# Attention scores as three rounded products, keys split on GpSimd, exponentials scaled on ScalarE

## The chip, the cores and the metric

One core of one Trainium2 chip runs the whole program. The metric is the time of one execution on the device, in microseconds (us). A core has TensorE (matrix products, PE), VectorE (DVE), ScalarE (ACT), GpSimd (POOL) and the queue of SyncE (SP), which here issues every DMA. Each engine runs its own program in order; a wait holds everything behind it on that engine.

## The reference, cut to what matters

The program is a two-layer block over 8 sequences of 100 tokens, 1024 wide, with a context of 361 tokens each. Layer 0: cross attention (16 query heads, 4 key heads, 96 wide; keys are the 361 context tokens and the 100 tokens themselves, 461 in all), then a feed-forward. Layer 1: cross attention (32 query heads, 8 key heads, 128 wide, queries and keys normalised, keys the 361 context tokens, a mask added), then a mixing of four streams. Each attention, cut:

```python
q = (latents @ Wq.T);  k = (hidden @ Wk.T);  v = (hidden @ Wv.T)
scores = jnp.einsum('bkgqd,bksd->bkgqs', q, k) * scale      # scale = HD ** -0.5
attn = jax.nn.softmax(scores.astype(jnp.float32), axis=-1)
out = jnp.einsum('bkgqs,bksd->bkgqd', attn, v);  return out @ Wo.T
```

## The kernel before

Stages follow each other: layer 1's context projections, layer 0's projections, `attend` for layer 0, a layer norm, the feed-forward, a layer norm, `attend` for layer 1, the mixing. The change is in `attend` (line 819) alone, which serves both layers.

**Two forms of product.** Large products are made of three rounded ones: an operand x is held as a rounded part `hi` (type float32r) and a remainder `lo` = x - hi, also rounded, and hi*hi + hi*lo + lo*hi is summed in PSUM (`product`, line 1267). The score product (line 1326), the turning of the probabilities (line 1337) and their product with the values (line 1346) are plain fp32. A plain fp32 product leaves two records in the trace, a rounded one leaves one.

**Tiles and units.** `attend` walks over units u: 32 in layer 0, 64 in layer 1. A unit is one batch and one key group, with four query heads; HB = 4 units share one key group and one half of the tokens. Query tiles (one 512 KB weight tile gives one product of 24 matmuls over 400 tokens) and output tiles (one per unit, two halves) come from DRAM through `w_raw` (RAW = 3 slots), are rounded by GpSimd into `w_hi` (line 1034) and their remainder made by VectorE in `w_lo` (line 1156), both with SPLIT = 4 slots. The first LEAD query products (6 in layer 0, 7 in layer 1) stand ahead of the units.

**The order, written out by hand.** In unit u TensorE runs: turns of chunks 0 and 1, scores of heads 0 and 1 of unit u + 2, the first half of the output product of unit u - 4, in layer 1 the sum of squares (lines 1304 and 1305), turns of the other chunks, the second half, scores of heads 2 and 3 of unit u + 2, once in four units in layer 1 the turning of the square sums (line 1311), the product with the values, and one query product (layer 0: in three of four units; none in the last units). Scores go to two PSUM banks, one per head of a pair, so a pair waits for the reader of the pair before: ScalarE's exponentials in layer 0 (line 1078), VectorE's scale-and-mask in layer 1 (line 1178).
ScalarE in unit u: copy of turned chunk 0 (line 1118), exponentials of heads 0 and 1 of unit u + 2 (line 1078 or 1081), copy of chunk 2, `copy_sums` (line 1105), exponentials of heads 2 and 3, `o_hi` (line 1140), roots (line 1111), `copy_q` (squares at line 1093, the query copy at line 1096).
VectorE in unit u: copy of chunk 1 (line 1203), maxima of the first pair (line 1166 or 1181), accumulating of the output halves (line 1211), maxima of the second pair, `normalise` of unit u + 1 (reciprocal at line 1189, four multiplies at line 1192), `o_lo` (line 1237), `q_scale` (line 1197), the weights' remainders for unit u + 1. In layer 0 the maxima are also multiplied by the score scale (`exp_bias`, line 1169), which is otherwise applied inside the exponential.
GpSimd in unit u: rounding of the weight tiles of unit u + 1, then in layer 1 the squares of the query product of unit u in two operations (lines 1043 and 1046), double buffered.
SP in unit u: keys and values of unit u + 3 (four slots, three DMAs, line 983 or 988 on) once unit u - 1 has read its values, then the weight tiles of unit u + 2, each once the remainder three tiles back is made.

## Time and profile before

| | |
|---|---|
| median of 3 runs | 2779.82 us (2779.24 to 2783.0) |
| the profiled execution | 2777.63 us, its span 2775.8 us |
| mean granted clock of TensorE | 0.949 of full speed |
| busy: PE, PEld, DVE, ACT, POOL | 91%, 76%, 52%, 30%, 19% |
| attention of layer 0 | from 839 to some 1335 us of the span |
| attention of layer 1 | from 1581 to some 2596 us |
| DMA | 217.4 MB, mean 78 GB/s |

The span is the time from the first to the last recorded instruction, 1.8 us less than the execution. PE is the matmul itself, PEld the load of its stationary operand, which the trace records beside it. A matmul's record is longer than the step to the next one, since matmuls are pipelined: steps are read from starts, or from one end to the next. In a timeline, "128*100 128x361" is stationary rows x columns and moving rows x columns; [1.99 <-DVE attend_p L1192] says how long the engine sat idle before and who ended it.

### The profile page before, as it was taken

The numbers are of one execution on the slowest core, as the hardware profiler recorded it, in microseconds if no ns is written. First come the engines' busy times: TensorE is split into PE (matmuls) and PEld (weight loads), VectorE is DVE, ScalarE is ACT, GpSimd is POOL, SyncE is SP. The second block draws the span as 40 slices with busy tenths as digits, with TensorE's granted clock in tenths as the row PEclk, the third lists the DMA queues.
The fourth block names the chain that finished last, engine by engine and source line by source line (L and its number), as shares of the span: only waits on it lengthen the run. The fifth ranks groups of instructions, "written<-read, shape, count | busy, mean of one in ns | idle before, by whom it ended". The sixth has DMA issues, their size and how long they took to land. (4 is left out here: it accounts for less than half of the span.)

```text
span 2775.8 us, 32483 instructions
## 1 busy us (share of the span) xinstructions
PE 2517.4 (91%) x12384; PEld 2109.7 (76%) x12384; DVE 1455.6 (52%) x2473; ACT 827.3 (30%) x1922; POOL 533.8 (19%) x414
## 2 busy tenths in 40 slices
PE   8999999799996899998769689999999999998824
PEld 6888888589995677776569468888888888886723
DVE  6222222223102576667543546666666766766697
ACT  3222222223212333333210234333333333332323
POOL 3000000000002122211021143334334334331120
PEclk9999999899997999999989889999999999999766
DMA  6222222253222222222021113323323223322001
GB/s 197 69 69 69 69 69 62 74 173 105 68 90 85 62 79 88 80 70 61 12 69 39 55 58 95 103 84 102 101 85 103 95 90 103 93 78 75 9 0 48
DMA packets 159357, 217.40 MB, mean 78 GB/s; under 512 B 31511, under 2 KB 124083, under 8 KB 158179
## 3 DMA queue, kind: packets, MB, share of 16 engines
q1 hardware_dynamic: 159202, 215.33, 25.4%
q8 instruction: 99, 1.62, 0.2%
q14 instruction: 56, 0.45, 0.1%
HBM read 176.99 MB, written 38.29 MB: 78 GB/s over the span
## 5 line engine op out<-in xcount | busy, mean ns | idle before, releaser
L1034 POOL TENSOR_TENSOR attend_w_hi<-attend_w_raw,attend_one 128x1024 fp32r<-128x1024 f32 (+1 forms) x184 | 335.9, 1840 | 478.6 <-DMA attend_w_raw<-in_wo 284.6
L1326 PE MATMUL attend_ps_score<-attend_k_in,attend_q 128*100 128x361 f32 (+1 forms) x768 | 298.1, 512 | 18.6 <-ACT attend_p L1078 11.0
L1271 PE MATMUL attend_ps_gemm<-normed_hi,attend_w_hi 128*128 128x400 f32 x704 | 268.3, 381 | 39.0 <-DVE attend_w_lo L1156 39.0
L1271 PE MATMUL attend_ps_gemm<-attend_o_hi,attend_w_hi 128*128 128x400 f32 x704 | 274.0, 389 | 27.0 <-DVE attend_w_lo L1156 24.5
L1156 DVE TENSOR_TENSOR attend_w_lo<-attend_w_raw,attend_w_hi 128x1024 fp32r<-128x1024 f32 (+1 forms) x184 | 216.7, 1212 | 155.8 <-POOL attend_w_hi L1034 154.8
L1081 ACT ACTIVATE attend_p<-attend_p,attend_neg_max 100x361 f32<-100x361 f32 x256 | 150.8, 590 | 398.0 <-DVE attend_neg_max L1181 398.0
L1271 PE MATMUL attend_ps_gemm<-attend_o_hi,attend_w_lo 128*128 128x400 f32 x704 | 244.7, 348 | 0.0
L1271 PE MATMUL attend_ps_gemm<-normed_lo,attend_w_hi 128*128 128x400 f32 x704 | 244.4, 347 | 0.0
L1271 PE MATMUL attend_ps_gemm<-attend_o_lo,attend_w_hi 128*128 128x400 f32 x704 | 244.2, 347 | 0.0
L1271 PE MATMUL attend_ps_gemm<-normed_hi,attend_w_lo 128*128 128x400 f32 x704 | 243.5, 346 | 0.0
L1211 DVE SCALAR_TENSOR_TENSOR stream_tokens<-attend_ps_gemm,attend_gate,stream_tokens 128x400 f32<-128x400 f32 x192 | 121.4, 633 | 230.3 <-PE attend_ps_gemm L1271 229.7
L1346 PE MATMUL attend_ps_out<-attend_pt,attend_v_in 121*128 121x400 f32 (+4 forms) x640 | 233.9, 503 | 0.0
L301 DVE TENSOR_TENSOR context_k_square<-context_k_rows 128x512 f32<-128x512 f32 (+1 forms) x46 | 31.8, 691 | 346.5 <-ACT context_k_rows L226 346.4
L1326 PEld LDWEIGHTS attend_ps_score<-attend_k_in,attend_q 128*100 128x100 f32 (+1 forms) x768 | 122.6, 171 | 93.2 <-issue 30.9
L1337 PEld LDWEIGHTS attend_ps_turn<-attend_ident,attend_p 100*121 100x121 f32 (+2 forms) x1280 | 167.3, 183 | 29.3 <-issue 9.6
L1346 PEld LDWEIGHTS attend_ps_out<-attend_pt,attend_v_in 121*128 121x128 f32 (+4 forms) x640 | 114.2, 180 | 98.1 <-issue 48.5
L1337 PE MATMUL attend_ps_turn<-attend_ident,attend_p 100*121 100x100 f32 (+2 forms) x1280 | 171.8, 271 | 7.4 <-DVE attend_p L1192 5.5
L1271 PEld LDWEIGHTS attend_ps_gemm<-normed_hi,attend_w_hi 128*128 128x128 f32 x704 | 134.0, 190 | 52.3 <-issue 43.3
L1271 PEld LDWEIGHTS attend_ps_gemm<-attend_o_hi,attend_w_hi 128*128 128x128 f32 x704 | 133.7, 190 | 50.6 <-DVE attend_w_lo L1156 39.7
L1043 POOL TENSOR_TENSOR attend_square_hi<-attend_q_square,attend_one 128x400 fp32r<-128x400 f32 x64 | 57.2, 893 | 550.9 <-ACT attend_q_square L1093 550.8
L350 PE MATMUL context_ps_rows<-context_wk_hi,context_ctx_hi 128*128 128x512 f32 (+1 forms) x368 | 145.9, 396 | 9.9 <-DVE context_wk_lo L294 9.9
L1178 DVE SCALAR_TENSOR_TENSOR attend_p<-attend_ps_score,attend_q_scale,attend_mask 100x361 f32<-100x361 f32 x256 | 147.7, 593 | 11.8 <-PE attend_ps_score L1326 4.6
(252 smaller groups left out, 5071.4 us busy)
## 6 DMA issues: line engine op xcount, KB each, us to landing
attend_w_raw<-in_wq SPq DMA_DIRECT2D x88, 512.0 KB, 3.8
attend_w_raw<-in_wo SPq DMA_DIRECT2D x64, 512.0 KB, 5.1
attend_w_raw<-in_wo SPq DMA_DIRECT2D x32, 384.0 KB, 3.5
context_ctx_raw<-in_ctxT SPq DMA_DIRECT2D x8, 1456.0 KB
attend_k_in<-scratch_k SPq DMA_DIRECT2D x64, 180.5 KB
context_ctx_raw<-in_ctxF SPq DMA_DIRECT2D x22, 512.0 KB
scratch_v<-context_v_out SPq DMA_DIRECT2D x44, 256.0 KB, 2.2
scratch_k<-context_kt_out SPq DMA_DIRECT2D x44, 256.0 KB, 5.0
```

The lines of the kernel that those rows point to most:

```text
L301: dve.tensor_tensor(k_square[:n], part, part, ALU.mult).then_inc(squared, 1)
L350: mm = pe.matmul(ps_rows[:n, m % ROW_BANKS], x[:, t % CTX, c, 0:n], w[:, c, col], start=(c == 0 and x is ctx_hi and w is w_hi), stop=(c == ...
L1034: pool.tensor_tensor(hi, w_flat(w_raw, j % RAW, j), one[:hi.shape[0]].to_broadcast(hi.shape), ALU.mult).then_inc(w_hi_done, 1)
L1043: pool.tensor_tensor(square_hi[:, n % 2], q_square[:], one[:HD].to_broadcast([HD, HT]), ALU.mult).then_inc(square_split, 1)
L1081: act.activation(p[:, slot, h], p[:, slot, h], ACT.Exp, bias=neg_max[:, slot, h:h + 1], accum_out=exp_sum[:, slot, h:h + 1]).then_inc(expe ...
L1156: dve.tensor_tensor(w_flat(w_lo, j % SPLIT, j), w_flat(w_raw, j % RAW, j), w_flat(w_hi, j % SPLIT, j).bitcast(F32), ALU.subtract).then_inc ...
L1178: dve.scalar_tensor_tensor(p[:, slot, h], ps_score[:S, h % 2, :NK], q_scale[:, i % 2, k, h:h + 1], mask[:], ALU.mult, ALU.add).then_inc(s_ ...
L1211: dve.scalar_tensor_tensor(tokens[:, m, at], ps_gemm[:, gemm_at["o", u, half] % 2, :HT], gate[:], tokens[:, m, at], ALU.mult, ALU.add).the ...
L1271: mm = pe.matmul(out, left[a](c), right[b](c), start=(c == 0 and a == b == 0), stop=(c == chunks - 1 and a == 1))
L1326: pe.matmul(ps_score[:S, h % 2, :NK], q[:, i % 2, h, k * S:(k + 1) * S], k_in[:, u % KV_SLOTS], start=True, stop=True).then_inc(s_done, 1)
L1337: turn = pe.transpose(ps_turn[:ROWS[kc], kc % 2, h * S:(h + 1) * S], p[:, u % P_SLOTS, h, at:at + ROWS[kc]], ident[:S, :S])
L1346: mm = pe.matmul(ps_out[:HD, :HG * S], v_in[:ROWS[kc], u % KV_SLOTS, kc], pt[:ROWS[kc], u % 2, kc], start=(kc == 0), stop=(kc == NCH - 1))
```

## The change

Scores become three rounded products (hi*hi, hi*lo, lo*hi) over one column more than there are keys (362 and 462, the last one zero and never read). ScalarE rounds the queries as it copies them (`q_hi`), VectorE makes their remainder (`remainder_q`), at the end of the unit; the PSUM bank of a query product is free only after it. In layer 0 the score scale goes into both, so the exponential has neither scale nor `exp_bias`. GpSimd splits the keys in two operations (`split_keys`), ahead of the unit's weights. The four multiplies of `normalise` go from VectorE to ScalarE, behind the copy of chunk 2; VectorE keeps the reciprocal (`invert`), now behind its copy of chunk 1. Slots: weights split 3 rather than 4, raw weights 3 in layer 0 and 2 in layer 1, keys 2, values 3, squares 1. Keys and values have DMAs and waits of their own. Declarations and semaphores are left out below.

```diff
--- before.py
+++ after.py
...
+    NKE = NK + 1
...
-    RAW, SPLIT = 3, 4
-    P_SLOTS, KV_SLOTS = 3, 4
-    KV_DMAS = 3
+    RAW, SPLIT = 3 - layer, 3
+    P_SLOTS, K_SLOTS, V_SLOTS = 3, 2, 3
+    V_DMAS = 2
...
-        q = sb("q", [HD, 2, HG, HT])
+        q_hi = sb("q_hi", [HD, 2, HG, HT], F32R)
+        q_lo = sb("q_lo", [HD, 2, HG, HT], F32R)
...
-        k_in = sb("k_in", [HD, KV_SLOTS, NK])
-        v_in = sb("v_in", [KR, KV_SLOTS, NCH, HD])
+        k_raw = sb("k_raw", [HD, K_SLOTS, NKE])
+        k_hi = sb("k_hi", [HD, K_SLOTS, NKE], F32R)
+        k_lo = sb("k_lo", [HD, K_SLOTS, NKE], F32R)
+        v_in = sb("v_in", [KR, V_SLOTS, NCH, HD])
...
-        exp_bias = sb("exp_bias", [S, P_SLOTS, HG])
...
-            square_hi = sb("square_hi", [HD, 2, HT], F32R)
-            square_lo = sb("square_lo", [HD, 2, HT], F32R)
+            square_hi = sb("square_hi", [HD, HT], F32R)
+            square_lo = sb("square_lo", [HD, HT], F32R)
...
+            def keys(u):
...
+                b, slot = batch(u), u % K_SLOTS
+                if u >= K_SLOTS:
+                    sp.wait_ge(k_lo_done, u - K_SLOTS + 1)
+                src = k_dram[g][:, b, :] if layer == 0 else k_dram[g][:, b * KEYS:(b + 1) * KEYS]
+                sp.dma_start(k_raw[:, slot, 0:NK], src).then_inc(k_load[slot], 16)
...
+            def values(u):
...
+                b, slot = batch(u), u % V_SLOTS
+                if u >= V_SLOTS:
+                    sp.wait_ge(pv_done, u - V_SLOTS + 1)
...
-            for u in range(KV_SLOTS - 1):
-                kv(u)
+            for u in range(K_SLOTS):
+                keys(u)
+            for u in range(V_SLOTS - 1):
+                values(u)
...
+            keys(K_SLOTS)
             for u in range(NU):
-                kv(u + KV_SLOTS - 1)
+                keys(u + K_SLOTS + 1)
+                values(u + V_SLOTS - 1)
                 for j in step_tiles(u + 2):
                     tile(j)
...
+            pool.memset(k_raw[:, :, NK:NKE], 0.0).then_inc(consts, 1)
...
+            def split_keys(u):
+                if u >= NU:
+                    return
+                slot = u % K_SLOTS
+                pool.wait_ge(k_load[slot], (u // K_SLOTS + 1) * 16)
+                if u >= K_SLOTS:
+                    pool.wait_ge(s_done, (u - K_SLOTS + 1) * HG)
+                pool.tensor_tensor(k_hi[:, slot], k_raw[:, slot], one[:HD].to_broadcast([HD, NKE]), ALU.mult
+                                   ).then_inc(k_hi_done, 1)
+                pool.wait_ge(k_hi_done, u + 1)
+                pool.tensor_tensor(k_lo[:, slot], k_raw[:, slot], k_hi[:, slot].bitcast(F32), ALU.subtract
+                                   ).then_inc(k_lo_done, 1)
...
-                if n >= 2:
-                    pool.wait_ge(q_summed, n - 1)
-                pool.tensor_tensor(square_hi[:, n % 2], q_square[:], one[:HD].to_broadcast([HD, HT]), ALU.mult
+                if n:
+                    pool.wait_ge(q_summed, n)
+                pool.tensor_tensor(square_hi[:], q_square[:], one[:HD].to_broadcast([HD, HT]), ALU.mult
                                    ).then_inc(square_split, 1)
                 pool.wait_ge(square_split, 2 * n + 1)
-                pool.tensor_tensor(square_lo[:, n % 2], q_square[:], square_hi[:, n % 2].bitcast(F32), ALU.subtract
+                pool.tensor_tensor(square_lo[:], q_square[:], square_hi[:].bitcast(F32), ALU.subtract
                                    ).then_inc(square_split, 1)
...
             for j in range(LEAD):
                 weights(j)
                 if j >= SPLIT - 1:
                     squares(j - SPLIT + 1)
+            split_keys(0)
             for n in range(LEAD - SPLIT + 1, LEAD):
                 squares(n)
+            split_keys(1)
             for j in step_tiles(0):
                 weights(j)
+            split_keys(2)
             for u in range(NU):
+                split_keys(u + 3)
                 for j in step_tiles(u + 1):
                     weights(j)
                 squares(query_of(u))
...
-                act.wait_ge(biased if layer == 0 else maxed, 2 * u + pair + 1)
...
-                        act.activation(p[:, slot, h], ps_score[:S, h % 2, :NK], ACT.Exp, bias=exp_bias[:, slot, h:h + 1],
-                                       scale=SCALE, accum_out=exp_sum[:, slot, h:h + 1]).then_inc(exped, 1)
+                        act.activation(p[:, slot, h], ps_score[:S, h % 2, :NK], ACT.Exp, bias=neg_max[:, slot, h:h + 1],
+                                       accum_out=exp_sum[:, slot, h:h + 1]).then_inc(exped, 1)
...
+            def normalise(u):
+                if u >= NU:
+                    return
+                slot = u % P_SLOTS
+                act.wait_ge(inverted, u + 1)
+                for h in range(HG):
+                    act.activation(p[:, slot, h], p[:, slot, h], ACT.Copy, scale=exp_inv[:, slot, h:h + 1]
+                                   ).then_inc(p_ready, 1)
...
-                act.activation(q[:, i % 2, h], ps_gemm[:HD, bank, :HT], ACT.Copy).then_inc(q_read, 1)
                 if layer == 0:
-                    act.activation(q[h * REST:(h + 1) * REST, i % 2, HG - 1], ps_gemm[HD:P, bank, :HT], ACT.Copy
-                                   ).then_inc(q_read, 1)
+                    act.activation(q_hi[:, i % 2, h], ps_gemm[:HD, bank, :HT], ACT.Copy, scale=SCALE).then_inc(q_read, 1)
+                    act.activation(q_hi[h * REST:(h + 1) * REST, i % 2, HG - 1], ps_gemm[HD:P, bank, :HT], ACT.Copy,
+                                   scale=SCALE).then_inc(q_read, 1)
+                else:
+                    act.activation(q_hi[:, i % 2, h], ps_gemm[:HD, bank, :HT], ACT.Copy).then_inc(q_read, 1)
...
-            for u in range(2):
-                exps(u, 0)
-                exps(u, 1)
+            exps(0, 0)
+            exps(0, 1)
+            exps(1, 0)
+            normalise(0)
+            exps(1, 1)
             for u in range(NU):
                 i, k = u // HB, u % HB
                 copy_turn(u, 0)
                 exps(u + 2, 0)
                 copy_turn(u, 2)
+                normalise(u + 1)
                 if layer == 1 and k == 1 and u + HB < NU:
                     copy_sums(i + 1)
                 exps(u + 2, 1)
...
+            def remainder_q(n):
+                if n is None:
+                    return
+                i, h = n // QT, n % QT
+                bank = gemm_at["q", n, 0] % 2
+                dve.wait_ge(q_read, (n + 1) * Q_COPIES)
+                if layer == 0:
+                    last = slice(h * REST, (h + 1) * REST)
+                    dve.scalar_tensor_tensor(q_lo[:, i % 2, h], ps_gemm[:HD, bank, :HT], SCALE,
+                                             q_hi[:, i % 2, h].bitcast(F32), ALU.mult, ALU.subtract).then_inc(q_lo_done, 1)
+                    dve.scalar_tensor_tensor(q_lo[last, i % 2, HG - 1], ps_gemm[HD:P, bank, :HT], SCALE,
+                                             q_hi[last, i % 2, HG - 1].bitcast(F32), ALU.mult, ALU.subtract
+                                             ).then_inc(q_lo_done, 1)
+                else:
+                    dve.tensor_tensor(q_lo[:, i % 2, h], ps_gemm[:HD, bank, :HT], q_hi[:, i % 2, h].bitcast(F32),
+                                      ALU.subtract).then_inc(q_lo_done, 1)
...
-                    dve.wait_ge(maxed, 2 * u + pair + 1)
-                    dve.tensor_scalar(exp_bias[:, slot, heads], neg_max[:, slot, heads], SCALE, None, ALU.mult
-                                      ).then_inc(biased, 1)
...
-            def normalise(u):
+            def invert(u):
...
                 dve.wait_ge(exped, (u + 1) * HG)
                 dve.reciprocal(exp_inv[:, slot], exp_sum[:, slot]).then_inc(inverted, 1)
-                dve.wait_ge(inverted, u + 1)
-                for h in range(HG):
-                    dve.tensor_scalar(p[:, slot, h], p[:, slot, h], exp_inv[:, slot, h:h + 1], None, ALU.mult
-                                      ).then_inc(p_ready, 1)
...
-            for j in range(LEAD):
+            for j in range(SPLIT):
                 split(j)
+            for j in range(SPLIT, LEAD):
+                remainder_q(j - SPLIT)
+                split(j)
+            for n in range(LEAD - SPLIT, LEAD):
+                remainder_q(n)
             if layer == 1:
                 scales(0)
             for j in step_tiles(0):
                 split(j)
-            for u in range(2):
-                maxima(u, 0)
-                maxima(u, 1)
-            normalise(0)
+            maxima(0, 0)
+            maxima(0, 1)
+            maxima(1, 0)
+            invert(0)
+            maxima(1, 1)
             for u in range(NU):
                 i, k = u // HB, u % HB
                 copy_turn(u, 1)
+                invert(u + 1)
                 maxima(u + 2, 0)
                 if u >= HB:
                     accumulate(u - HB, 0)
...
                 maxima(u + 2, 1)
-                normalise(u + 1)
...
                 for j in step_tiles(u + 1):
                     split(j)
+                remainder_q(query_of(u))
...
-                        pe.wait_ge(q_read, (at + 1) * Q_COPIES)
+                        pe.wait_ge(q_lo_done, (at + 1) * Q_COPIES)
...
-                    pe.wait_ge(kv_load[u % KV_SLOTS], (u // KV_SLOTS + 1) * 16 * KV_DMAS)
+                    pe.wait_ge(k_lo_done, u + 1)
                     if k == 0:
-                        pe.wait_ge(q_read, (i + 1) * QT * Q_COPIES)
+                        pe.wait_ge(q_lo_done, (i + 1) * QT * Q_COPIES)
...
-                    pe.matmul(ps_score[:S, h % 2, :NK], q[:, i % 2, h, k * S:(k + 1) * S], k_in[:, u % KV_SLOTS],
-                              start=True, stop=True).then_inc(s_done, 1)
+                    at = slice(k * S, (k + 1) * S)
+                    for a, b in ((q_hi, k_hi), (q_hi, k_lo), (q_lo, k_hi)):
+                        mm = pe.matmul(ps_score[:S, h % 2, :NKE], a[:, i % 2, h, at], b[:, u % K_SLOTS],
+                                       start=(a is q_hi and b is k_hi), stop=(a is q_lo))
+                    mm.then_inc(s_done, 1)
...
+                pe.wait_ge(v_load[u % V_SLOTS], (u // V_SLOTS + 1) * 16 * V_DMAS)
```

## Rows read from the trace of the kernel before

**Rows 1.** The page, part 1: busy us (share) xinstructions of each engine.

```profile
PE 2517.4 (91%) x12384; PEld 2109.7 (76%) x12384; DVE 1455.6 (52%) x2473; ACT 827.3 (30%) x1922; POOL 533.8 (19%) x414
```

**Rows 2.** Busy us of PE, PEld, DVE, ACT, POOL by stretch; clock; DMA.

```profile
970.00:1240.00 270.00, 266.14 (x1288) 205.43 (x1287) 189.57 (x356) 103.30 (x293) 54.61 (x33) 1.00 0.28 82
1700.00:2500.00 800.00, 799.78 (x4114) 678.93 (x4112) 548.19 (x925) 296.46 (x751) 295.98 (x212) 1.00 0.30 94
```

**Rows 3.** TensorE's waits, and who ended them: us, times, longest.

```profile
PE attend_ps_gemm L1271 <- DVE attend_w_lo L1156: 63.5, 19, 25.9
```

**Rows 4.** Timeline, units of layer 1: start us, us, engine, line, operation.

```profile
2008.22 0.99 PE L1337 MATMUL attend_ps_turn<-attend_ident,attend_p 100*121 100x100 f32 x8
...
2008.83 0.50 ACT L1096 ACTIVATE attend_q<-attend_ps_gemm 128x400 f32<-128x400 f32 x1
...
2009.06 1.38 PE L1326 MATMUL attend_ps_score<-attend_k_in,attend_q 128*100 128x361 f32 x4
...
2009.26 0.57 DVE L1203 COPY attend_pt<-attend_ps_turn 121x400 f32<-121x400 f32 x1 [1.13 <-PE attend_ps_turn L1337]
...
2011.10 0.91 DVE L1181 TENSOR_REDUCE attend_neg_max<-attend_p 100x2 f32<-100x722 f32 x1
...
2013.84 0.48 ACT L1105 ACTIVATE attend_q_sum<-attend_ps_sum 4x400 f32<-4x400 f32 x1
...
2016.76 0.35 PE L1311 MATMUL attend_ps_sum<-attend_ident,attend_q_sum 4*100 4x4 f32 x4
...
2486.10 0.99 PE L1337 MATMUL attend_ps_turn<-attend_ident,attend_p 100*121 100x100 f32 x8
```

**Rows 5.** Timeline, a pair of scores of layer 0, the product ahead.

```profile
1002.52 0.34 PE L1271 MATMUL attend_ps_gemm<-attend_o_hi,attend_w_lo 128*128 128x400 f32 x1
1002.70 1.71 PE L1326 MATMUL attend_ps_score<-attend_k_in,attend_q 96*100 96x461 f32 x4
```

**Rows 6.** Timeline, rounded products of 512, 362 and 384 columns, first and last counted.

```profile
399.76 0.39 PE L350 MATMUL context_ps_rows<-context_wk_hi,context_ctx_hi 128*128 128x512 f32 x1
...
401.80 0.39 PE L350 MATMUL context_ps_rows<-context_wk_hi,context_ctx_hi 128*128 128x512 f32 x1
...
726.19 0.33 PE L765 MATMUL context_ps_out<-context_ctx_hi,context_wk_hi 128*128 128x362 f32 x1
...
729.83 0.33 PE L765 MATMUL context_ps_out<-context_ctx_lo,context_wk_hi 128*128 128x362 f32 x1
...
814.66 0.34 PE L765 MATMUL context_ps_out<-context_wv_hi,normed_hi 128*100 128x384 f32 x1
...
816.23 0.34 PE L765 MATMUL context_ps_out<-context_wv_hi,normed_hi 128*100 128x384 f32 x1
...
814.84 0.16 PEld L765 LDWEIGHTS context_ps_out<-context_wv_hi,normed_lo 128*100 128x100 f32 x1
```

**Rows 7.** Groups by line: xcount | busy us, mean ns | idle; exponentials.

```profile
L1081 ACT ACTIVATE attend_p<-attend_p,attend_neg_max 100x361 f32<-100x361 f32 x256 | 150.8, 590 | 398.0 <-DVE attend_neg_max L1181 398.0
```

**Rows 8.** The same groups, GpSimd's rounding of weights, remainder of squares.

```profile
L1034 POOL TENSOR_TENSOR attend_w_hi<-attend_w_raw,attend_one 128x1024 fp32r<-128x1024 f32 x152 | 288.8, 1917 | 255.4 <-DMA attend_w_raw<-in_wq 166.2 <-DMA attend_w_raw<-in_wo 63.0 <-PE attend_ps_gemm L1271 26.0
L1046 POOL TENSOR_TENSOR attend_square_lo<-attend_q_square,attend_square_hi 128x400 fp32r<-128x400 f32 x64 | 67.3, 1051 | 5.0
```

**Rows 9.** DMA issues: xcount, KB each, median us from issue to landing.

```profile
attend_w_raw<-in_wo SPq DMA_DIRECT2D x64, 512.0 KB, 5.1
```

**Rows 10.** Timeline, a unit without a query product ahead of it.

```profile
2498.40 1.38 PE L1326 MATMUL attend_ps_score<-attend_k_in,attend_q 128*100 128x361 f32 x4
...
2499.74 1.16 DVE L1156 TENSOR_TENSOR attend_w_lo<-attend_w_raw,attend_w_hi 128x1024 fp32r<-128x1024 f32 x1
```

**Rows 11.** Timeline, first scores and turns of layer 0, with idle ahead.

```profile
889.79 3.39 PE L1326 MATMUL attend_ps_score<-attend_k_in,attend_q 96*100 96x461 f32 x4 [2.18 <-ACT attend_p L1078]
...
895.17 2.44 PE L1337 MATMUL attend_ps_turn<-attend_ident,attend_p 100*121 100x100 f32 x8 [1.99 <-DVE attend_p L1192]
```

**Rows 12.** VectorE's split of the weights: duration ns min/median/max.

```profile
L1156 DVE TENSOR_TENSOR attend_w_lo<-attend_w_raw,attend_w_hi x184: 950/1215/2909, 845.4 to 2570.8; 128x1024 fp32r<-128x1024 f32 x152, 128x768 fp32r<-128x768 f32 x32
```

29 lines of the change are left out of this document (15 added, 14 removed).

## The prediction

> **What bounds the kernel now.** I read the page's busy times first: TensorE is busy 2517 us of 2776 [rows 1]. That is an average over stages, so next come the busy times by stretch. In the middle of layer 1's attention TensorE is busy 799.78 us of 800 at a granted clock of 1.00; in the middle of layer 0's, 266.14 of 270 [rows 2]. VectorE is at 69%, ScalarE at 37% and GpSimd at 37% in the 800 us. So each us taken out of TensorE's stream there is a us of the kernel, unless an in-order queue elsewhere turns late. The list of TensorE's waits says which: weights' remainders (line 1156), 63.5 us in 19 waits, one of 25.9 at the start of the stage, the rest in starts and in units without a query product [rows 3]. A unit is one batch and one key group; from the turns at 2008.22 to those of the 32nd unit after, at 2486.10, it takes 14.93 us [rows 4].
>
> **Scores, the large term.** Before, a head is one fp32 product, recorded as two. In layer 1 the turns end at 2008.22 + 0.99 = 2009.21 and the four records of a pair of heads at 2009.06 + 1.38 = 2010.44: 1.23 us a pair [rows 4]. In layer 0 (461 keys) the product ahead ends at 1002.52 + 0.34 = 1002.86 and the pair at 1002.70 + 1.71 = 1004.41: 1.55 us [rows 5].
> After, a head is three products of rounded operands, over 362 or 462 columns. No score runs so yet, but the same kind does in the projections. At 362 columns the starts go from 726.19 to 729.83 in 22 steps: 0.1655 us each; at 512, 399.76 to 401.80 in 9: 0.227; a line between them gives 0.206 at 462 [rows 6]. So a pair is 6 x 0.1655 = 0.99 us in layer 1 and 6 x 0.206 = 1.24 us in layer 0. Gain: 0.24 x 128 pairs = 30 us, of which I take 0.23 and 29 us, since starts are given to 0.01; and 0.31 x 64 pairs = 19.8 us. **Sum 48.8 us**. Between bounds: the 512 row's own price for layer 0 gives 1.36 a pair and 12 us; the 362 row's 0.99 gives 36.
> Here a rule speaks against the change. The rows show products with 100 stationary columns, rounded, over 384 moving ones, every 0.1744 us (814.66 to 816.23 in 9 steps), each with a weight load of its own [rows 6]. So the third load per head (one per record before) is hidden, and I add nothing.
> The Trainium skill, TensorE: Matmul & The Clock Gate, in its list of what overlaps under the measured speedup of tiles, has a weight load overlap a product in flight only where their row groups differ. By its section on LDWEIGHTS 100 columns would then cost 83 ns a product, and 1152 products an estimated 96 us, less those loads that fp32 exposes today. By that rule, these rows disagree.
>
> **Normalising moves from VectorE to ScalarE.** Four multiplies a unit leave VectorE. ScalarE gets four copies of 100x361: at most the exponential's 0.59 us on the same tile [rows 7], at least the 0.48 of a small copy [rows 4], less what neighbours overlap: some 2 us a unit, on an engine at 37%. What waits behind them counts: the second exponentials, which wait for later scores anyway, and in layer 1 once in four units the copy of the square sums, which TensorE reads to turn (line 1311). In the unit at 2008.22 it starts 5.6 us into the unit and TensorE arrives at 8.54 [rows 4]. After, the query remainder holds VectorE's turn copy by some 0.6, and through maxima and exponentials this copy too; then the four copies: start 8.2 to 8.7, end 8.6 to 9.2. TensorE arrives 0.46 earlier, at 8.08. Wait 0 to 1.1 us, taken 0.6, 15 times: **9 us given back** (0 to 17).
>
> **Query remainders on VectorE**, one per query product in layer 1, two in layer 0: 0.57 us each by the copy of the same size [rows 4]. VectorE loses 1.4 to 1.6 us of multiplies a unit against that. They sit at the unit's end and start once ScalarE has rounded, 1.1 us into the next unit, so VectorE's turn copy comes at 1.7 rather than 1.04, and the maxima of the first pair end near 4.4. TensorE asks for their buffers at 7.2: hidden. In layer 0, two exponentials end near 5.5 and are wanted at 6.4: hidden, by 1 us. The gemm bank is wanted two products on.
>
> **Keys split by GpSimd**: two operations a unit; over 128x400 the dearer of such operations costs 1.05 us [rows 8], so over 362 columns the two take at most 1.9, over 462 some 2.4. With two squares' operations at up to 1.05 and two weight tiles at 1.92 [rows 8] GpSimd goes from 5.9 of 14.9 us to 7.8 of 14.5. They are a whole unit ahead of the scores that read them. Behind them stand the weights of the next unit. With three rounded slots for four, the query tile's rounding now waits for the output product of the running unit, 7.2 us in; it ends at 9.1. VectorE splits it some 12 us into the unit, once the products' remainder is done: hidden by some 3 us.
>
> **One raw slot less (layer 1) and the loads.** On SP's queue the tile loads of a unit go out after VectorE's splits at the unit's end, land 5.1 us later [rows 9], and keys and values stand behind them. Keys, a third of the bytes, land 5 to 6 us into the next unit, their split ends near 8, the output tile's rounding near 10, the query tile's near 12: hidden by 1 to 3 us. Values have a unit and more; their three slots suffice, since a slot's reader is two units back.
>
> **Where the stream waits for a weight remainder anyway**, a quicker first pair gains nothing: in the unit at 2497 the scores end at 2499.78 and the remainder at 2500.90 [rows 10]. There are some 12 such units in layer 0 (8 first units of a token half, 4 at the end) and 5 in layer 1: 12 x 0.31 + 5 x 0.23 = **4.8 us back**.
>
> **Starts.** Layer 0's first score pairs run at about half clock, 3.39 us each with ScalarE between, and the first turns wait 1.99 for the multiplies [rows 11]. Four pairs at half clock save some 0.6 more than counted, the bias operation 0.2 each, the earlier normalising 1: **4 us gained** (0 to 6). Layer 1: the second key split (1.9 us) precedes the weight rounding for which the first maxima wait; half-clock scores save about half: **1 us lost**. Memset, reciprocal moved, squares in one buffer: nothing; the squares' readers come 1 us later than their writers today.
>
> Sum: -48.8 + 9 + 4.8 - 4 + 1 = -38 us. From the profiled execution's 2777.6, 2739.6; the runs' median is 2.2 above it, so **2742 us**.
>
> **Rivals.**
> A, *nothing given back* (2729 us, 2721 to 2733): ScalarE's copies take 0.4, so the square sums come in time; for it, neighbouring ScalarE rows overlap by 0.1. 48.8 + 4 - 1 = 52 at best.
> B, *ScalarE and VectorE run late* (2762, 2752 to 2775): the wait at line 1311 is 1.1 (8 us more) and layer 0's second pair waits 0.5 us for the first pair's exponentials in its 24 query units (12 more): 20 above the forecast. For it, the 1 us of slack.
> C, *the weight chain becomes the bound* (slower, 2799): in layer 1 with two raw slots the chain from one unit's split to the next is in series: landing 5.1, keys' landing 1.7 (a third of the bytes), key split 1.9, rounding 1.9, split 1.2: 11.8 of 14.5 us. But VectorE's split ran up to 2.91 rather than 1.2 beside a GpSimd operation [rows 12]. With 2.9 each for rounding and split and half as much again for the keys the chain is 15.5: 1.0 us a unit over 57 units, 57 us. It decides against the change from 15.2 on, where it takes back the 38. Against it: most splits took the median 1.215.
> The Trainium skill, SBUF — State Buffer, on the shared port pair, says that a VectorE operation with two SBUF inputs and a GpSimd operation that reads SBUF shut each other out for a whole instruction; the 2.91 agrees.
> D, *weight loads show* (2914): were each load's 0.16 us added [rows 6], a head would take 3 x (0.1655 + 0.16) = 0.98 for 0.615 in layer 1 (93 us more) and 1.10 for 0.775 in layer 0 (41 more).
> E, *the rounded product is not the quick form here*: no gain, within 0.2% of before.
>
> **Chances.** Forecast (2733 to 2752) 0.56, A 0.20, B 0.14, C 0.07, D 0.01, E 0.02. The range 2722 to 2765 takes in A and most of B. 0.2% (5.6 us) is about what a measurement of this kernel can tell from no change: faster 0.90, same 0.02, slower 0.08.
>
> **What would show it.** Score records 1152 for 768, starts 0.165 and 0.206 apart; layer 1's unit near 14.5 us; a TensorE wait at the turning of the square sums; first-pair stalls on weight remainders longer by 0.2 to 0.3. Wrong if TensorE's busy share in 1700 to 2450 falls under 97% with GpSimd or the weight remainder named, or if the records stand 0.2 apart in layer 1.

## The result, and the profile after

The changed kernel takes **2770.66 us** (median of 8 runs, 2768.73 to 2776.78) against 2779.65 (8 runs, 2777.85 to 2783.0) for the kernel before: ratio 0.9968, 95% interval 0.9958 to 0.9977. It is faster by 9 us; the forecast was 38, and 2770.66 lies above the range of 2722 to 2765. The profiled execution spans 2766.9 us, against 2775.8 before.

From the page, busy times of the engines:

```profile
PE 2489.0 (90%) x12768; PEld 2191.2 (79%) x12768; DVE 1335.7 (48%) x2137; ACT 1018.3 (37%) x2306; POOL 714.3 (26%) x608
```

TensorE's busy time fell by 28 us, the span by 9. Busy times by stretch as in [rows 2], PE, PEld, DVE, ACT, POOL, then the clock, then the DMA:

```profile
970.00:1240.00 270.00, 263.65 (x1405) 225.96 (x1405) 163.63 (x278) 149.46 (x375) 97.69 (x74) 0.99 0.29 84
1700.00:2500.00 800.00, 794.91 (x4432) 728.60 (x4431) 500.86 (x787) 405.53 (x991) 402.43 (x328) 1.00 0.32 98
```

TensorE's waits, as in [rows 3], more of the list: total in us, times, longest.

```profile
PE attend_ps_gemm L1338 <- DVE attend_w_lo L1206: 74.6, 22, 24.6
...
PE attend_ps_gemm L1338 <- DVE stream_tokens L1271: 7.8, 2, 4.3
...
PE attend_ps_sum L1378 <- ACT attend_q_sum L1152: 3.9, 3, 3.6
```

The wait for weight remainders grew from 63.5 us in 19 [rows 3]. The scores themselves did what was forecast. TensorE's timeline, a pair of layer 1 and the product behind it:

```profile
2004.56 0.99 PE L1407 MATMUL attend_ps_turn<-attend_ident,attend_p 100*121 100x100 f32 x8
2005.33 0.39 PE L1395 MATMUL attend_ps_score<-attend_k_hi,attend_q_hi 128*100 128x362 f32 x1
2005.55 0.32 PE L1395 MATMUL attend_ps_score<-attend_k_lo,attend_q_hi 128*100 128x362 f32 x1
...
2006.20 0.32 PE L1395 MATMUL attend_ps_score<-attend_k_hi,attend_q_lo 128*100 128x362 f32 x1
2006.37 0.35 PE L1338 MATMUL attend_ps_gemm<-attend_o_hi,attend_w_hi 128*128 128x400 f32 x1
```

From the second on, the starts are 0.16 apart; the turns end at 2005.55, the pair at 2006.52: 0.97 us for the forecast 0.99. A steady unit of layer 1 takes 14.38 us for 14.84 before.

**Where the rest went** is seen by cutting both traces at the first and the last turns of each layer. Layer 0's units (31 between them) take 427.1 us for 429.4; layer 1's (63) take 891.5 for 908.0. Behind the first turns of each layer's last unit more time passes than before: in layer 0 to the start of the feed-forward stage 80.3 for 72.5 us, in layer 1 to the first product of the mixing 39.8 for 35.2. So layer 0 gained 2.3 us in its units and lost 7.8 behind them.

The trace shows what happens in the units; what stands behind them is taken up with e1_slots. TensorE's timeline in a unit of layer 0 behind one without a query product:

```profile
1260.12 0.37 PE L1395 MATMUL attend_ps_score<-attend_k_hi,attend_q_lo 96*100 96x462 f32 x1
1262.07 0.45 PE L1338 MATMUL attend_ps_gemm<-attend_o_hi,attend_w_hi 128*128 128x400 f32 x1 [1.58 <-DVE attend_w_lo L1206]
...
1262.73 0.36 PE L1338 MATMUL attend_ps_gemm<-attend_o_hi,attend_w_hi 128*128 128x400 f32 x1
1262.91 0.52 PE L1338 MATMUL attend_ps_gemm<-attend_o_lo,attend_w_hi 128*128 128x400 f32 x1
1263.22 0.54 PE L1338 MATMUL attend_ps_gemm<-attend_o_hi,attend_w_lo 128*128 128x400 f32 x1
1263.56 0.54 PE L1338 MATMUL attend_ps_gemm<-attend_o_hi,attend_w_hi 128*128 128x400 f32 x1
...
1266.35 0.35 PE L1338 MATMUL attend_ps_gemm<-attend_o_lo,attend_w_hi 128*128 128x400 f32 x1
1266.54 0.34 PE L1338 MATMUL attend_ps_gemm<-attend_o_hi,attend_w_lo 128*128 128x400 f32 x1
```

The same place in the kernel before:

```profile
1267.28 0.45 PE L1271 MATMUL attend_ps_gemm<-attend_o_hi,attend_w_hi 128*128 128x400 f32 x1 [0.94 <-DVE attend_w_lo L1156]
1267.57 0.34 PE L1271 MATMUL attend_ps_gemm<-attend_o_lo,attend_w_hi 128*128 128x400 f32 x1
1267.75 0.34 PE L1271 MATMUL attend_ps_gemm<-attend_o_hi,attend_w_lo 128*128 128x400 f32 x1
```

Two things changed. The stall grew from 0.94 to 1.58 us, and from 1262.91 on, 0.84 us behind its end, the products start 0.33 apart for 0.18: TensorE is at 1.2 GHz for some 3.4 us. That unit takes 13.53 us where the ones without the drop take 11.92 and the same unit before 12.22. So the stall gives back one pair's gain, and a drop 1.6 us more. Of the ten such stalls in layer 0, five are followed by a drop. From 838 to 1350 us TensorE has 83.7 us at half clock, for 51.2 before. Of the 32.5 us more, 17 stand behind those five stalls and most of the rest at the layer's end.

### The profile page after: what moved, and what is told of

It is laid out like the page before. It is cut to its first block and busy times, and to the rows that moved or that the text cites. A ratio compares the mean times of both kernels' runs of the same rounds, so it can differ in the third digit from the quotient of the medians.

```text
span 2766.9 us, 33590 instructions
## 1 busy us (share of the span) xinstructions
PE 2489.0 (90%) x12768; PEld 2191.2 (79%) x12768; DVE 1335.7 (48%) x2137; ACT 1018.3 (37%) x2306; POOL 714.3 (26%) x608
## 5 line engine op out<-in xcount | busy, mean ns | idle before, releaser
L1338 PE MATMUL attend_ps_gemm<-attend_o_hi,attend_w_hi 128*128 128x400 f32 x704 | 259.0, 368 | 44.7 <-DVE attend_w_lo L1206 36.9
L1417 PE MATMUL attend_ps_out<-attend_pt,attend_v_in 121*128 121x400 f32 (+4 forms) x640 | 239.8, 514 | 0.0
L1126 ACT ACTIVATE attend_p<-attend_p,attend_exp_inv 100x361 f32<-100x361 f32 (+1 forms) x384 | 207.4, 616 | 0.0
L1063 POOL TENSOR_TENSOR attend_k_hi<-attend_k_raw,attend_one 128x362 fp32r<-128x362 f32 (+1 forms) x96 | 81.1, 845 | 445.1 <-DMA attend_k_raw<-scratch_k 291.7
L1395 PE MATMUL attend_ps_score<-attend_k_hi,attend_q_hi 128*100 128x362 f32 (+1 forms) x384 | 141.8, 369 | 21.2 <-ACT attend_p L1114 13.3
L1303 DVE TENSOR_TENSOR attend_o_lo<-attend_ps_out,attend_o_hi 128x400 fp32r<-128x400 f32 (+1 forms) x96 | 51.7, 539 | 216.2 <-ACT attend_o_hi L1190 119.9
```

What stands on the lines that cost most here:

```text
L1063: pool.tensor_tensor(k_hi[:, slot], k_raw[:, slot], one[:HD].to_broadcast([HD, NKE]), ALU.mult).then_inc(k_hi_done, 1)
L1126: act.activation(p[:, slot, h], p[:, slot, h], ACT.Copy, scale=exp_inv[:, slot, h:h + 1]).then_inc(p_ready, 1)
L1303: dve.tensor_tensor(o_lo[:HD, i % 2, :, k * S:(k + 1) * S], ps_out[:HD, :QT * S].rearrange("p (h t) -> p h t", h=QT), o_hi[:HD, i % 2, :, ...
L1338: mm = pe.matmul(out, left[a](c), right[b](c), start=(c == 0 and a == b == 0), stop=(c == chunks - 1 and a == 1))
L1395: mm = pe.matmul(ps_score[:S, h % 2, :NKE], a[:, i % 2, h, at], b[:, u % K_SLOTS], start=(a is q_hi and b is k_hi), stop=(a is q_lo))
L1417: mm = pe.matmul(ps_out[:HD, :HG * S], v_in[:ROWS[kc], u % V_SLOTS, kc], pt[:ROWS[kc], u % 2, kc], start=(kc == 0), stop=(kc == NCH - 1))
```

## The experiments

Ratios are to the kernel before, with their 95% intervals; its median stood at 2779.65 in the runs above and at 2781.26, 2781.23, 2780.70 and 2780.73 in the four sets below. Experiments of different sets are compared with the changed kernel by ratio. The ratios are those on record; the quotients of the medians differ from them by up to 0.0006 (1.6 us). One execution of each kernel was traced, so a difference of one or two us in a single trace can be the clock's.

| label | median us | ratio | 95% |
|---|---|---|---|
| e1_slots | 2789.54 | 1.0025 | 1.0016 to 1.0034 |
| e2_normalise | 2787.44 | 1.0020 | 1.0011 to 1.0029 |
| e3_fp32 | 2795.43 | 1.0048 | 1.0035 to 1.0062 |
| e4_early | 2723.81 | 0.9788 | 0.9774 to 0.9801 |
| e5_before_early | 2758.31 | 0.9917 | 0.9903 to 0.9930 |
| e6_filler | 2755.82 | 0.9911 | 0.9897 to 0.9924 |
| e7_sums | 2716.38 | 0.9766 | 0.9752 to 0.9779 |
| e8_tail | 2717.13 | 0.9770 | 0.9756 to 0.9783 |
| e9_all | 2712.39 | 0.9750 | 0.9735 to 0.9764 |
| e10_defer | 2709.82 | 0.9741 | 0.9726 to 0.9755 |
| e11_fp32_early | 2757.01 | 0.9909 | 0.9893 to 0.9926 |
| e12_stall | 2799.12 | 1.0064 | 1.0050 to 1.0077 |

### Parts of the change alone: e1_slots, e2_normalise, e3_fp32

```diff
--- e1_slots, on the kernel before
-    RAW, SPLIT = 3, 4
+    RAW, SPLIT = 3 - layer, 3
...
```

> The kernel before with three rounded weight slots for four in both layers and two raw ones for three in layer 1, nothing else. Theory 'fewer slots delay the stage ends': the last output tiles wait for a product's slot, TensorE's last waits grow from 1.1 and 1.3 us to some 3.4 and 4.3, and with them the tails: 5 to 12 us slower than the kernel before. Rival 'slots hidden', as the prediction had it: within 2 us. Rival 'the layer 1 loads come late too': more than 20 us slower, with weight waits inside layer 1's steady units.

0.25% of 2780 is 7 us slower: the first theory. Steady units are as before (14.85), so the third rival falls. GpSimd's timeline at the end of layer 0, then TensorE's:

```profile
1347.99 1.47 POOL L1034 TENSOR_TENSOR attend_w_hi<-attend_w_raw,attend_one 128x768 fp32r<-128x768 f32 x1 [11.22 <-PE attend_ps_gemm L1271]
```

```profile
1351.26 0.67 PE L1271 MATMUL attend_ps_gemm<-attend_o_hi,attend_w_hi 128*128 128x400 f32 x1 [3.42 <-DVE stream_tokens L1211]
```

In the kernel before that rounding was released by the load, not by a product:

```profile
1342.04 1.47 POOL L1034 TENSOR_TENSOR attend_w_hi<-attend_w_raw,attend_one 128x768 fp32r<-128x768 f32 x1 [9.07 <-DMA attend_w_raw<-in_wo]
```

With three slots the last tile waits until the last but three is multiplied. The trace puts the stall down to the accumulation (line 1211); the changed kernel, with stalls of 3.42 us in layer 0 and 4.33 in layer 1 (where e1_slots has 5.95), shows what was late. Its timeline at the end of layer 1, GpSimd, VectorE, TensorE:

```profile
2555.23 2.23 POOL L1053 TENSOR_TENSOR attend_w_hi<-attend_w_raw,attend_one 128x1024 fp32r<-128x1024 f32 x1 [0.77 <-PE attend_ps_gemm L1338]
2557.50 1.22 DVE L1206 TENSOR_TENSOR attend_w_lo<-attend_w_raw,attend_w_hi 128x1024 fp32r<-128x1024 f32 x1 [1.78 <-POOL attend_w_hi L1053]
2558.65 1.17 DVE L1271 SCALAR_TENSOR_TENSOR stream_tokens<-attend_ps_gemm,attend_gate,stream_tokens 128x400 f32<-128x400 f32 x2
...
2559.42 0.42 PE L1338 MATMUL attend_ps_gemm<-attend_o_hi,attend_w_hi 128*128 128x400 f32 x1 [4.33 <-DVE stream_tokens L1271]
```

VectorE's queue has all four splits ahead of the accumulations, so the accumulation that frees TensorE's bank stands behind a split that waits for a late rounding. The slots alone account for what layer 0 loses behind its units: from the first turns of its last unit to the layer norm's first product it is 40.3 us here, 40.4 in the changed kernel and 32.6 before. Half clock from 1310 us to that product is 20.5 us in both, for 6.8 before.

```diff
--- e2_normalise, on the kernel before (ScalarE's order; VectorE keeps the reciprocal, behind copy_turn(u, 1))
                 copy_turn(u, 2)
+                normalise(u + 1)
...
```

> The kernel before with the normalising alone moved to ScalarE, in the changed kernel's order. The prediction's step: waits at the turning of the square sums of 0.6 us 15 times (9 us) less what the starts gain, so 5 us slower. By the trace of the changed kernel the waits are 0.46 us, so about 4 us slower, within 2 us. Rival 'ScalarE is where the gain went': 15 us or more slower. Rival 'free': the same within 1 us.

0.20%: 5.6 us slower, near the forecast of 5, but not where the forecast had it. The units in which the square sums are turned take 15.31 us as before: no wait there in steady state. The loss is in layer 1's second unit (16.36 for 12.71, a wait of 2.9 us at the turning with half clock behind it), partly offset by its first (11.93 for 13.55), in layer 0's first two units (33.8 for 31.9) and in layer 1's last (11.68 for 9.74). And the stall on the weight remainder is 1.29 us, not 0.94, at an equal unit length of 12.22. The reason shows in the turns ahead of it. The kernel before, TensorE and its weight loads:

```profile
1263.45 1.33 PE L1337 MATMUL attend_ps_turn<-attend_ident,attend_p 100*121 100x100 f32 x8
...
1264.01 0.60 PEld L1337 LDWEIGHTS attend_ps_turn<-attend_ident,attend_p 100*121 100x121 f32 x5 [0.19 <-DVE attend_p L1192]
```

and e2_normalise:

```profile
1264.57 0.99 PE L1346 MATMUL attend_ps_turn<-attend_ident,attend_p 100*121 100x100 f32 x8
```

VectorE's multiplies used to hold the turns back by 0.34 us. Freed, TensorE comes that much earlier to a remainder that is no earlier.

```diff
--- e3_fp32, on the changed kernel
-                    for a, b in ((q_hi, k_hi), (q_hi, k_lo), (q_lo, k_hi)):
-                        mm = pe.matmul(ps_score[:S, h % 2, :NKE], a[...], b[...], ...)
+                    mm = pe.matmul(ps_score[:S, h % 2, :NK], q_hi[...].bitcast(F32), k_hi[...].bitcast(F32),
+                                   start=True, stop=True)
```

> The changed kernel with each score one fp32 product of the rounded halves again (it leaves out the remainders' part of the scores), all else kept. If rounded scores are worth the predicted 48.8 less 4.8 in this order of work: 2813 to 2817 us. If layer 0's share is given back through stalls (weight remainders and the clock behind them), only layer 1's 57 units of 0.46 count: 26 us, 2795 to 2800. If the gain in layer 1 is lost as well: below 2785.

Everything but the rounded scores costs 0.48%, 13.4 us, of which slots (7.0) and normalising (5.6) alone make 12.6: keys on GpSimd and the query remainders are free within the intervals. The rounded scores are worth 1.0048 - 0.9968, 22 us, in the changed kernel: the second theory's size or a little less. The stalls are 1.28 to 1.29 us here, and none of the ten brings a drop.

### The late remainder: e4_early and e5_before_early

VectorE sits idle ahead of o_lo while the rounded weights have been ready for long. VectorE's rows in the changed kernel:

```profile
1259.69 0.47 DVE L1303 TENSOR_TENSOR attend_o_lo<-attend_ps_out,attend_o_hi 96x300 fp32r<-96x300 f32 x1 [2.82 <-ACT attend_o_hi L1194]
...
1261.06 0.96 DVE L1206 TENSOR_TENSOR attend_w_lo<-attend_w_raw,attend_w_hi 128x768 fp32r<-128x768 f32 x1
```

```diff
--- e4_early, on the changed kernel (e5_before_early: the same, on the kernel before)
                 maxima(u + 2, 1)
+                early = step_tiles(u + 1)[:1] if u + 1 >= HB else []
+                for j in early:
+                    split(j)
                 dve.wait_ge(o_hi_done, (u + 1) * O_COPIES)
...
-                for j in step_tiles(u + 1):
+                for j in step_tiles(u + 1)[len(early):]:
                     split(j)
```

> The changed kernel with VectorE's remainder of the next output tile placed ahead of its wait for ScalarE's rounded outputs, not behind. Theory 'the chain from values through o_hi and o_lo to the weight remainder bounds the units without a query product, and stalls of 1.6 us bring half clock': the 1.58 us waits fall to 0.4 to 0.7, the half-clock stretches behind them go away, 15 to 25 us faster than the changed kernel: 2746 to 2756. Rival 'the clock drops for another reason': only the waits shrink, 16 x 1.0: 2754 to 2760 with the half-clock stretches still there. Rival 'the wait moves to another engine': within 4 us of 2771.

It is 0.0180 of 2780, 50 us, faster than the changed kernel by ratio (the two traces differ by 44), twice what was expected. VectorE's rows in e4_early, one unit:

```profile
1256.56 0.95 DVE L1206 TENSOR_TENSOR attend_w_lo<-attend_w_raw,attend_w_hi 128x768 fp32r<-128x768 f32 x1
...
1259.46 0.47 DVE L1306 TENSOR_TENSOR attend_o_lo<-attend_ps_out,attend_o_hi 96x300 fp32r<-96x300 f32 x1 [1.96 <-ACT attend_o_hi L1194]
```

and TensorE's waits there:

```profile
PE attend_ps_gemm L1341 <- DVE attend_w_lo L1206: 37.7, 2, 24.8
...
PE attend_ps_turn L1410 <- DVE attend_pt L1263: 5.8, 10, 2.0
```

Twenty of 22 waits are gone from this list (at the layers' last tiles waits of 2.7 and 1.25 us stay, which the trace puts down to no engine), and units with output products only take 10.09 us in layer 0 for 11.92 or 13.53, 9.63 in layer 1 for 11.15. What I had left out of the expectation: a remainder that isn't late gives back all of the stall, and the half clock, and the pair that the stall used to swallow. The units of layer 0, first to last turns, take 400.6 us for 427.1, layer 1's 881.5 for 891.5.

> The kernel before with the same reordering as e4_early and nothing of the change: the remainder of the next output tile ahead of VectorE's wait for the rounded outputs. It has 17 waits of some 0.94 us there, so it gains 16 to 19 us and comes to 2762 to 2766. The change is then worth about 38 to 42 us between the two reordered kernels, as the prediction's sum had it, and what the change lost was lost to the weight remainders. Rival 'the reordering is as good for either kernel': it too gains 47 us, 2734, and the change is worth only 9 whatever the order.

22.9 us faster than the kernel before, a little more than expected. Between the two reordered kernels the change is worth 2758.31 - 2723.81 = **34.5 us**: near the sum of 38. The second rival (9 whatever the order) falls.

### The clock: e6_filler and e12_stall

```diff
--- e6_filler, on the changed kernel, ahead of the wait for w_lo in outputs()
                 if half == 0:
+                    if layer == 0 and query_of(u + HB - 1) is None and u + HB > HB:
+                        for _ in range(7):
+                            pe.matmul(ps_sum[:, :HT], ln_hi[:, 0, 0:P], ln_hi[:, 0, 0:HT], start=True, stop=True)
                     pe.wait_ge(w_lo_done, j + 1)
```

> The changed kernel with seven extra rounded products (about 1.2 us, into a bank that layer 0 does not use) in each of layer 0's stalls of 1.58 us on a weight remainder; no wait is taken away. Theory 'the stall brings the half clock': the half-clock stretches behind those stalls go away and the kernel is 12 to 18 us faster than the changed one (2753 to 2759) though it does more work. Rival 'the half clock has another cause': as many half-clock stretches, within 2 us of 2771 or slower.

16 us faster by ratio (0.0057), with more work. The condition holds in 16 places, and the trace has 112 filler products: seven ahead of each of the ten stalls, and as many in each of six places at the layer's end. TensorE's timeline:

```profile
1254.85 1.43 PE L1358 MATMUL attend_ps_sum<-normed_hi 128*128 128x400 f32 x7
1256.58 0.45 PE L1338 MATMUL attend_ps_gemm<-attend_o_hi,attend_w_hi 128*128 128x400 f32 x1 [0.31 <-DVE attend_w_lo L1206]
1256.88 0.35 PE L1338 MATMUL attend_ps_gemm<-attend_o_lo,attend_w_hi 128*128 128x400 f32 x1
1257.06 0.34 PE L1338 MATMUL attend_ps_gemm<-attend_o_hi,attend_w_lo 128*128 128x400 f32 x1
```

The product behind the wait starts no earlier in its unit (3.82 us behind the turns in both), but no half-clock products follow, in none of the ten places; half clock in the stage falls from 83.7 to 51.2 us, as before the change. Half of the difference is 16 us, about the gain. But not all of that is the price of the drops behind the ten stalls. The traces differ by 8 us in the five units that had a drop (1.6 each), by some 6 at the layer's end (1.6 in its last unit, 4.7 behind it), where e1_slots has as much half clock as the changed kernel, and by less than 1 elsewhere. The stretch 1240 to 1300 us in the changed kernel and in e6_filler, columns as above:

```profile
1240.00:1300.00 60.00, 53.14 (x250) 41.77 (x248) 30.25 (x54) 34.46 (x88) 15.62 (x13) 0.91 0.19 50
```

```profile
1240.00:1300.00 60.00, 58.40 (x308) 47.04 (x307) 34.10 (x60) 35.48 (x93) 17.09 (x14) 1.00 0.23 64
```

```diff
--- e12_stall, on the kernel before, VectorE
                 dve.wait_ge(o_hi_done, (u + 1) * O_COPIES)
+                if layer == 0 and u >= HB and query_of(u) is None:
...
+                    for t in range(2):
+                        dve.tensor_tensor(waste[:, t, 0:QT * S], ps_out[:HD, :QT * S], one[:HD].to_broadcast([HD, QT * S]),
+                                          ALU.mult).then_inc(waste_done, 1)
```

> The kernel before with two extra VectorE products (96x300, about 0.47 us each, into a tile that nothing reads) between ScalarE's rounded outputs and the weight remainder, in layer 0's 13 units without a query product. The 10 waits of 0.94 us become some 1.9 us, with nothing of the change in the kernel. Theory 'a longer stall lowers the clock': half-clock stretches of 3.4 us stand behind most of them, each 1.6 us dearer than the wait alone: 13 x 0.95 = 12 us and 7 to 10 times 1.6, together 24 to 28 us, 2804 to 2809. Rival 'the clock falls by what the change computes, not by the stall': 10 to 13 us slower only, 2791 to 2794, with the half-clock time in layer 0 as before.

18 us slower: between the two. The stalls are 1.70 us, for 0.94, in all ten places (0.76 each, 10 us over 13 units), but in the profiled execution only two of the ten were followed by a drop; the longer ones at the stage's end (3.25, 3.59 and 4.42 us) all were, and half clock rose from 51.2 to 71.7 us (here up to 1363 us, since the stage ends later). TensorE's rows, first without a drop behind it, then with one:

```profile
1301.40 0.45 PE L1281 MATMUL attend_ps_gemm<-attend_o_hi,attend_w_hi 128*128 128x400 f32 x1 [1.70 <-DVE attend_w_lo L1159]
...
1314.37 0.52 PE L1281 MATMUL attend_ps_gemm<-attend_o_hi,attend_w_hi 128*128 128x400 f32 x1 [1.70 <-DVE attend_w_lo L1159]
```

So stalls bring the drops without anything of the change, but the length alone doesn't settle one near 1.6 us. Fewer drops came than the theory had forecast. What else decides there is open.

### The other terms: e7_sums, e8_tail, e11_fp32_early

```diff
--- e7_sums, on e4_early, ScalarE
-                normalise(u + 1)
                 if layer == 1 and k == 1 and u + HB < NU:
                     copy_sums(i + 1)
+                normalise(u + 1)
```

> e4_early with ScalarE's copy of the square sums ahead of its normalising, not behind. The prediction gave 9 us to this wait at the turning of the square sums; the trace of the changed kernel shows 0.46 us at 13 places. Theory: 5 to 8 us faster than e4_early, 2716 to 2719. Rival 'the wait moves to the next reader' (the exponentials or the maxima behind them): within 1.5 us of 2724.

7.4 us faster, of which the traces place 5.7. Units that turn the square sums take 14.83 us for 15.05 (14 times, 3 us), and layer 1's second unit 14.81 for 17.55. That unit was the dearest single spot. The 0.46 us in the expectation is the step from the product ahead to the turning, not a wait: TensorE is idle there for 0.14 us, and the step is 0.25 in e7_sums (0.40 in the kernel before). TensorE's rows in it, in the kernel before and in the changed one:

```profile
1664.74 0.35 PE L1311 MATMUL attend_ps_sum<-attend_ident,attend_q_sum 4*100 4x4 f32 x4 [0.96 <-ACT attend_q_sum L1105]
```

```profile
1667.31 0.50 PE L1378 MATMUL attend_ps_sum<-attend_ident,attend_q_sum 4*100 4x4 f32 x4 [3.55 <-ACT attend_q_sum L1152]
1667.74 1.04 PE L1417 MATMUL attend_ps_out<-attend_pt,attend_v_in 121*128 121x400 f32 x1
```

There the four copies sit between the sums and their reader while no output products cover them, and half clock follows (1.04 us for the first product, which takes 0.60 in the kernel before).

```diff
--- e8_tail, on e4_early: the last 2 * HB tiles take slots out of four, the fourth in the query buffers
+            if j == len(tiles) - 2 * HB:
+                users[SPLIT] = -SPLIT
...
+            flat = w[:, slot] if slot < SPLIT else spare[:, 0].rearrange("p h t -> p (h t)")
...
+                elif slots[j][0] == SPLIT:
+                    pool.wait_ge(s_done, (NU - HB) * HG)
```

> e4_early with a fourth rounding slot for the last eight output tiles of each layer, in the half of the query buffers whose scores are done. Theory 'the missing slot delays the stage ends': the last waits of TensorE in each layer shrink by some 2 to 3 us, 4 to 8 us faster than e4_early, 2716 to 2720. Rival 'the loads of the last tiles bound the end, not the slots': within 1.5 us of 2724.

6.7 us faster, what e1_slots had lost. Layer 0's stall on the accumulation is gone; layer 1's stays at 4.37 us, so there the rounding slot is not the last cause. GpSimd's rows in e8_tail show the last rounding of layer 1 released by the load of its tile, where the changed kernel had a product:

```profile
2502.79 2.36 POOL L1067 TENSOR_TENSOR attend_w_hi<-attend_w_raw,attend_one 128x1024 fp32r<-128x1024 f32 x1 [0.65 <-DMA attend_w_raw<-in_wo]
```

Layer 1 has two raw slots for three, but that wasn't tried alone.

> e4_early with each score one fp32 product of the rounded halves (it leaves out the remainders' part of the scores). The size of the score term by itself, in an order of work in which no weight remainder is late: by the unit lengths of e4_early and e5_before_early (14.85 to 14.38 in layer 1, 15.04 to 14.45 and 10.66 to 10.09 in layer 0) 57 x 0.46 + 28 x 0.58 = 42 us more than e4_early, 2763 to 2769. By the prediction's own figure with nothing taken back, 48.8: 2772. If TensorE gains less because VectorE or ScalarE already bound it: under 2755.

(Its edits are e4_early's and e3_fp32's.) The score term by itself is 2757.01 - 2723.81 = **33.2 us**: below the 42 of the unit lengths and the 48.8 of the sum. First to last turns, layer 1 gains 21.7 us, layer 0 10.7. Steady units do gain 0.45 and 0.57. What is missing lies where a unit waits for something else: 14 units of layer 1 at the square sums (0.24 for 0.46), five of layer 0 at VectorE's turn copy (0.28 for 0.57), and the first four units of layer 0, which are 2.5 us longer rather than shorter, on half clock (60.7 for 58.2). Two of these 2.5 may be the clock's alone: e3_fp32 has the same order in these units as e11_fp32_early and takes 60.4.

### The version that beats both: e9_all, e10_defer

> The version meant to beat both: the changed kernel with the three edits together (output tile's remainder early, square sums copied ahead of the normalising, the spare slot for the last tiles). If they are independent, 7.4 and 6.7 us off e4_early's 2723.8: 2709 to 2711. If they share a stretch: 2713 or more.

2712.39: 11.4 us under e4_early, for the 14.1 of e7 and e8 together. The 2.7 us between are within the intervals (0.9735 to 0.9764 here), so it is not shown that the two gains overlap.

```diff
--- e10_defer, on e9_all, VectorE
                 copy_turn(u, 1)
+                if u:
+                    remainder_q(query_of(u - 1))
                 invert(u + 1)
...
                     split(j)
-                remainder_q(query_of(u))
```

> e9_all with the query remainder on VectorE behind the first turn copy of the next unit, not ahead of it. e4_early shows TensorE waiting for VectorE's turn copy 5.8 us in 10, and layer 0's second units of a token half 15.07 against 14.45. Theory 'the remainder holds the turn copy up': 3 to 4 us faster than e9_all. Rival 'the remainder comes late for its own bank or for the maxima behind it': 5 us slower or more. Rival 'no matter': within 1.5 us.

2.6 us faster by the medians, between the theory's 3 to 4 and none, but with intervals that overlap; and layer 0's units in question are as long as before (15.06), so the mechanism I gave isn't the one. The traces differ by 3.0 us between layer 0's last turns and layer 1's first, 2.6 of them in the layer norms and the feed-forward, which the edit doesn't touch. A gain from this edit is not shown. **2709.82 us** is 2.6% below the kernel before and 2.3% below the changed one.

## Why the prediction was wrong

Faster, as forecast with 0.90, but by 9 us for 38.

- **Score price**: right to the size. 0.97 us a pair in layer 1 for 0.99 (1.04 from the first start to the next product's), a steady unit 0.46 shorter for 0.46; layer 0 0.57 for 0.62. Loads cost nothing visible, so rivals D and E fall. As to the Trainium skill, "TensorE: Matmul & The Clock Gate", in its list "What overlaps and what doesn't": by that rule the scores would have been slower than before; here starts 0.16 apart with a load each disagree with it. The price times the pairs was too much all the same: with no remainder late the whole term is 33.2 us for 48.8 (e11_fp32_early), since a shorter unit meets other waits, which the sum had at nothing.
- **"Where the stream waits for a weight remainder anyway", 4.8 us**: this is the step that failed. I counted there the gain that such a unit can't use, expected stalls 0.2 to 0.3 us longer, and put their growth at nothing otherwise. Without a drop that count holds: 11.92 and 16.28 us for 12.22 and 16.59, one pair. But the stalls grew by 0.64 to 1.58 us, 0.35 of it from the normalising (e2_normalise) and 0.30 from the scores, and five of ten then brought some 3.4 us at half clock: 1.6 us each, 8 us in the trace. e6_filler gets 16 us back, 8 of them there and some 6 at the layer's end, where the slots have their part. e4_early and e5_before_early show that most of the shortfall hangs on the late remainders: with them out of the way the change is worth 34.5 us for 9. Of these 25.5 us the score term takes 11 (33.2 for 22). The rest is in the other parts, which cost 13.4 us in this order and nothing there (e11_fp32_early stands 1.3 us under e5_before_early).
- **"With three rounded slots for four ... hidden"**: wrong at the layers' ends, where only output tiles are left and no query tile's slot lies between. 7 us (e1_slots), a term of its own that I had put at nothing. In steady state it is hidden, as said.
- **Wait at the turning of the square sums, 9 us**: 7.4 (e7_sums), a near size by luck, since it isn't 0.6 us 15 times: 3 us in 14 units and 2.7 in one, the second of layer 1, which I had not looked at by itself. e2_normalise has no such wait in steady state, so the normalising alone doesn't bring it; whether the earlier TensorE or the later maxima do was not tried.
- **Starts, 4 us gained and 1 lost**: layer 0 reaches its first turns 1.9 us sooner, and its first four units are 2 us longer; layer 1 reaches them 4.2 sooner, and its second unit is 4.8 longer. What a start gained was gone again a few units later; the clock has a part in it, as said under e11_fp32_early.
- **Keys on GpSimd, query remainders**: hidden, as forecast (e3_fp32: 13.4 us for all other parts, 12.6 of them slots and normalising). Rival C (two raw slots, chain bound) falls: TensorE is busy 794.91 of 800 us. So does rival A (nothing given back).

By terms, in us, in the order of work that the change has: scores less what stalls swallow, -44 forecast, -22 measured; normalising and starts +6, +5.6 (by luck: the loss stands in other units than forecast); slots 0, +7; the rest 0, +1. The forecast missed 22 and 7. The measured 2770.66 lies within rival B's 2752 to 2775, but not by B's causes: TensorE's wait for ScalarE's exponentials is 13.3 us in 8, for 11.0 in 7 before.

## What to carry to other kernels

Before counting a gain on the busiest engine, list each place where it already waits for an in-order chain, and ask what the stall will be afterwards, not only what it swallows: a stall that grows can cost more than its growth. Where a tuned kernel's engine idles ahead of one wait with other ready work queued behind it, moving that work ahead can be worth more than faster arithmetic: here 23 us alone and 50 behind the change, which gave 9 by itself. Check slot counts at a stage's end apart from its steady state, since the mix of tiles is another there.

## What the runs showed of the hardware that was not expected

Short stalls in a busy stream can be followed by TensorE's half clock (1.2 GHz for 2.4). In layer 0 the 10 stalls of 0.94 us of the kernel before and the 20 of 1.28 to 1.29 us of e2_normalise and e3_fp32 had none behind them; of the 10 of 1.58 to 1.60 us in the changed kernel 5 had, of the 10 of 1.70 us in e12_stall 2. These drops lasted 3.4 us and began 0.2 to 1.0 us behind the stall's end. Of the 21 stalls of 2.5 to 4.4 us at the layer's end in these kernels and e1_slots, 19 had half clock beside or behind them, for 3.4 to 6.8 us. Seven products that nobody reads, set in each stall, kept the clock at 2.4 GHz behind all ten and, with those at the layer's end, made the kernel 16 us faster.

Why 1.70 us brought fewer drops than 1.58 wasn't settled. The work around the stalls differs between the two kernels, each count comes from one execution, and the count need not be the same in each: over the eight runs of the changed kernel the mean granted clock goes from 0.940 (2768.73 us) to 0.935 (2776.78 us).
